# Projection products of 512 columns cut into halves of 256 columns, in a retention and FFN kernel on one core

## The reference

```python
def attention(x, Wq, Wk, Wv, Wg, Wo, gn_weight):      # H = 4 heads, q and k 64 wide, v 128 wide
    q, k = apply_rotary(heads(x @ Wq), heads(x @ Wk))  # x @ Wq and x @ Wk: 256 columns each
    v = heads(x @ Wv)                                  # 512 columns
    o = chunk_retention(q * 64 ** -0.5, k, v, gamma)   # causal, decays by gamma per token
    g = silu(x @ Wg)                                   # 512 columns
    return (rmsnorm(o, gn_weight) * g) @ Wo

def ffn(x, w_gate, w_up, w_down):                      # int weights * 1/127, hidden width 768
    return (silu(x @ w_gate.T) * (x @ w_up.T)) @ w_down.T

x = layernorm(x + attention(x, ...))
x = layernorm(x + ffn(x, ...))
```

## Time and profile before

| what | value |
|---|---|
| median of the 3 runs | 449.24 us |
| the profiled execution: its time, its span | 449.29 us, 447.6 us |
| granted TensorE clock, mean | 0.999 |
| TensorE matmul busy | 434.5 us (97%) |
| TensorE weight loads busy (beside the matmuls) | 392.7 us (88%) |
| VectorE, ScalarE, GpSimd busy | 69%, 60%, 54% |

### The profile page before, as it was taken

The page is one execution under the profiler, slowest core; times in us unless marked ns, Lnnn a source line. Parts: engine busy times, 40 slices in busy tenths (PEclk is TensorE's granted clock), DMA queues, the critical chain, the costliest instruction groups (busy, mean ns, idle before and its releaser), DMA issues.

```text
span 447.6 us, 10332 instructions
## 1 busy us (share of the span) xinstructions
PE 434.5 (97%) x3288; PEld 392.7 (88%) x3288; DVE 307.6 (69%) x785; ACT 269.3 (60%) x794; POOL 241.3 (54%) x381
## 2 busy tenths in 40 slices
PE   8989999999999999999999999999999999999994
PEld 3877889999999999999999999999999999999983
DVE  3989565677666677666768667577766667765774
ACT  5778766566655566654666556556665556665541
POOL 2654355655655466554666436665565536554564
PEclk9999999999999999999999999999999999999999
DMA  7911010010100101010010202002010100100011
GB/s 244 349 42 49 0 49 1 1 61 13 61 12 26 34 12 59 12 59 12 19 39 12 59 12 59 0 12 59 12 59 12 35 1 12 37 14 12 14 38 38
DMA packets 15932, 18.45 MB, mean 41 GB/s; under 512 B 1440, under 2 KB 13728, under 8 KB 15904
## 3 DMA queue, kind: packets, MB, share of 16 engines
q1 hardware_dynamic: 15904, 18.09, 12.7%
HBM read 13.89 MB, written 4.19 MB: 40 GB/s over the span
## 4 chain that ended last, share of the span: by engine, by line
PE 87%; DVE 6%; issue 2%; POOL 1%; ACT 1%; DMA 1%; SPq 0%; POOLq 0%; DVEq 0%; ACTq 0%
PE b_rows L399 44%; PE b_ffn L399 18%; PE b_head L496 6%; PE b_state L399 3%; PE b_head L464 3%; PE b_head L467 3%; PE b_turn L412 3%; PE b_turn L522 3%; PE b_ffn L485 2%; DMA wf_int<-in_w_proj 1%; DVE y L1095 1%; DVE qk L1012 1%; DVE rot_s L999 1%; POOL h_lo L1262 1%; DVE rot_c L992 1%
## 5 line engine op out<-in xcount | busy, mean ns | idle before, releaser
L1262 POOL TENSOR_TENSOR h_lo<-wf_int,h_hi 128x256 fp32r<-128x256 f32 x96 | 71.4, 743 | 61.4 <-ACT h_hi L822 61.0
L399 PE MATMUL b_ffn<-x1T_hi,wf_hi 128*128 128x256 f32 x384 | 92.7, 278 | 0.6 <-DVE x1T_lo L1074 0.6
L399 PE MATMUL b_ffn<-x1T_lo,wf_hi 128*128 128x256 f32 x384 | 91.8, 276 | 0.0
L399 PE MATMUL b_rows<-wp_hi,xT_hi 128*128 128x512 f32 x186 | 78.8, 424 | 0.0
L399 PEld LDWEIGHTS b_ffn<-x1T_hi,wf_hi 128*128 128x128 f32 x384 | 72.1, 188 | 3.9 <-DVE x1T_lo L1074 1.1
L399 PEld LDWEIGHTS b_ffn<-x1T_lo,wf_hi 128*128 128x128 f32 x384 | 72.1, 188 | 2.8
L1287 POOL TENSOR_TENSOR ve<-mv,eps 128x1 f32<-128x1 f32 x64 | 14.1, 221 | 111.7 <-DVE mv L1116 103.9
L399 PE MATMUL b_rows<-wp_hi,xT_lo 128*128 128x512 f32 x186 | 73.4, 395 | 0.0
L399 PE MATMUL b_rows<-wp_lo,xT_hi 128*128 128x512 f32 x186 | 73.3, 394 | 0.0
L786 ACT ACTIVATE sq<-b_head 128x128 f32<-128x128 f32 x124 | 34.5, 278 | 57.2 <-PE b_head L496 54.3
L1107 DVE TENSOR_TENSOR z<-b_rows,x_sb 128x256 f32<-128x256 f32 x32 | 13.6, 424 | 67.0 <-PE b_rows L399 67.0
(11 more groups left out here) (112 smaller groups left out, 1078.2 us busy)
## 6 DMA issues: line engine op xcount, KB each, us to landing
xT_raw<-in_xT SPq DMA_DIRECT2D x16, 256.0 KB, 3.1
x_sb<-in_x SPq DMA_DIRECT2D x16, 256.0 KB, 2.7
out<-wf_int SPq DMA_DIRECT2D x32, 128.0 KB, 1.7
wf_int<-in_w_ffn SPq DMA_DIRECT2D x6, 384.0 KB, 7.0
wf_int<-in_w_proj SPq DMA_DIRECT2D x6, 256.0 KB, 4.8
rope_sb<-in_rope SPq DMA_DIRECT2D x4, 256.0 KB, 6.6
wo_raw<-in_w_o SPq DMA_DIRECT2D x1, 512.0 KB, 7.6
gn_sb<-in_gn SPq DMA_DIRECT2D x1, 0.5 KB, 7.0
```

The source lines that it names most:

```text
L399: mm = pe.matmul(dst, a, b, start=(i == 0 and j == 0 and not begun), stop=(i == n - 1 and j == len(passes) - 1 and not more), skip_group_c ...
L1262: pool.tensor_tensor(h_lo[:, ring, hb], h_full[:, u], h_hi[:, ring, hb].bitcast(F32), ALU.subtract).then_inc(h_split[j], 1)
```

## The change

A new function issues the six passes of a projection. Its first `whole` passes are made over all 512 columns, as before. The other passes are made first for columns 0 to 255 and then for columns 256 to 511. `whole` is 3 for q and k, 0 for v and 3 for g. Slot 0 keeps its own branch.

```diff
+            def projection_passes(dst, stat, mov, whole):
+
+                passes = [(sh if st == 0 else sl, mh if mt == 0 else ml)
+                          for (sh, sl), (mh, ml) in zip(stat, mov) for st, mt in ((0, 0), (0, 1), (1, 0))]
+                n = len(passes)
+                for i in range(whole):
+                    a, b = passes[i]
+                    pe.matmul(dst[:], a, b, start=i == 0, stop=False, skip_group_check=True)
+                for cols in (slice(0, 256), slice(256, 512)):
+                    for i in range(whole, n):
+                        a, b = passes[i]
+                        mm = pe.matmul(dst[:, cols], a, b[:, cols], start=i == 0, stop=i == n - 1,
+                                       skip_group_check=True)
+                return mm
...
                 else:
-                    mm = split_product(dst[:], stat, mov)
+                    mm = projection_passes(dst, stat, mov, (3, 0, 3)[c])
                 mm.then_inc(done, 1)
```

## The result

The changed kernel takes 452.97 us (median of 5 runs, 452.81 to 453.36) against 449.11 us before: a ratio of 1.0083, interval 1.0072 to 1.0094. It is 3.9 us slower, where 2.2 us less had been forecast. Its profiled span is 451.2 us.

The account below looks back on a forecast made before the run. TensorE's matmul stream was taken to bound the kernel: 27 slots x 0.080 = 2.16 us, plus some 0.04 from the first slots, made 2.2 us less, 449.24 - 2.2 = 447.0 us. The range was 446.0 to 449.2.

Parts of the forecast that it names:

- What bounds the kernel: From the first slots on, TensorE's stream of matmuls sets the time; TensorE is busy 97% of the span.
- the first term: In each slot's projections, 12 cut passes at 226.7 ns for two halves against 233.3 whole: 0.080 us gained a slot.
- The size of a cut at the fast pace: In q and k, v and g: timeline gains of 0.02, 0.04 and 0.03 us a slot, together 0.09.
- The part about the drain: The drain at the end has no projection and shifts as a whole.
- Extra weight loads at nothing: The 372 added weight loads in the projections hide behind the pass before them; unhidden, 0.19 us each, 70 us in all.
- The wait for `x1T_split`: Rival: at FFN block 0 a later VectorE chain takes up to all 2.2 us, leaving 449.2 us; chance 0.07.
- the loop's code: Rival: the longer loop body no longer fits on chip, four jumps back fetch, up to 6.8 us, 453.8; chance 0.04.
- the surcharge of the operands: Rival: projection passes' 20 ns belong to their operands: by column 449.2 us, chance 0.06; by instruction 455.7, chance 0.06.
- its turning point: At L417, the halves: the operand surcharge turns the change to slower from 116.7 ns a half on.
- The rule of the Trainium skill: Warm matmuls every N / 2.4 ns and 2.5 ns: two halves 218.3 against 215.8 ns, 0.8 us lost.

Follow-up runs that it names:

- v_only: Changed kernel with all six passes of q and k and of g whole, so only v in halves: 448.65 us, 0.9974 of the kernel before.
- v_and_g: Changed kernel with all six passes of q and k whole, v and g cut as in the change: 447.58 us, 0.9950 of the kernel before.
- v_one_whole: Changed kernel with the first pass of v whole, its other five in halves: 451.90 us, 1.0047 of the kernel before.
- qk_only: Changed kernel with all passes of v and g whole, so only q and k cut: 453.04 us, 1.0067 of the kernel before.
- qk_wide_end: Changed kernel with the last of q and k's six passes whole again, behind two passes in halves: 453.49 us, 1.0097 of the kernel before.
- qk_1_whole: Changed kernel with 1 instead of 3 whole passes in q and k: 452.98 us, 1.0088 of the kernel before.
- fifth_turn: Changed kernel with a fifth matmul in the turn of q and k, repeating the fourth block: 450.92 us, 1.0032 of the kernel before.

## Why the prediction was wrong

- **What bounds the kernel:** right. TensorE's stream sets the time before and after, and the loss from slot 7 to the last turn is in the spacing of its matmuls.
- **The step that failed** is the first term, "By the spacings, a slot gains 12 x (233.3 - 226.7) = 0.080 us". It took 113.3 ns as the cost of a narrow pass wherever it stands, and with that took for granted that the passes behind the halves keep their cost. In the change 52 narrow passes of a slot (46 without a state update) run at 117.7, that is 18 halves and 34 passes that nobody touched. 52 x 4.4 = 0.23 us more, against 0.08 less, gives 0.15, and the slot grew by 0.14. Over four slots, with 12.55 us in place of 12.44 in the fourth, it is 0.13 a slot. It holds for 25 slots and not for 27: at q and k of slot 7 the changed kernel is 0.15 us ahead of the one before (76.35 against 76.51 us), behind the last turn of q and k it is 3.19 behind (412.10 against 408.91). These 3.34 us are most of the 3.65 between the two profiled spans. Another 0.46 lie behind the last matmul, on the other engines; that tail took 6.4 to 7.7 us in the traces looked at, so they are not put down to the change.
- **The size of a cut at the fast pace** was right: 0.04 us a slot for v's six and 0.02 for g's three, as v_only and v_and_g showed. With a whole-pass count that keeps the fast pace, the kernel does come out at 447.0 to 447.6 us, which is what had been forecast for 3, 0, 3. The part about the drain was right too: from the last turn of q and k to the last matmul it is 32.10 us in both traces.
- **Extra weight loads at nothing:** held in v_only, with 186 more of them and a gain. Weight loads are busy 414.2 instead of 392.7 us, 21.5 more and not 14. In v_and_g, at the fast pace, 279 more loads made 11.7 us more (404.4), which would be 15.6 for 372. The other 6 are about what some 1300 narrow passes take longer at 4.4 ns each, an estimate: in a narrow stream the loads run nearly throughout.
- **The wait for `x1T_split` and the loop's code:** right that neither mattered. There is no new wait, and the loop's later rounds fetched no instructions (DMA table, 144 to 358 us, the only row with a queue):

```profile
q1 hardware_dynamic: 6656, 6.29, 9.5%
```

- **The rivals:** the surcharge of the operands came nearest, and its turning point, 116.7 ns a half, was passed. But its mechanism fails: the same operands ran at 113 ns in nine runs, and passes with other operands slowed down as much. None of the rivals had the true one, a cost to passes that the change leaves alone, so the range ended at 449.2.
- **The rule of the Trainium skill** in "TensorE: Matmul & The Clock Gate", section "Back-to-back issue gap", forecast a loss, and a loss came, but not that one. By it a narrow pass is 109.2 ns and two halves lose 2.5 ns to a wide pass; here they won 6.7 at the fast pace and lost 2.1 at the slow one. The prediction also took the rule too widely: that section gives it for a single matmul by itself, and says that a stream of weight loads and matmuls has a spacing of its own.

**What stays open:** why a narrow stream has two paces, and by what state of TensorE the pace is chosen. Shown is only that it is fixed where the stream begins, that it depends on the matmuls before (in slots 7 to 31 on their number behind the turn of q and k, in slot 6 on something from further back), that neither the moved waits nor the other order of passes changed it, that the same halves' operands ran at either pace, that the place in the program doesn't decide (slots 28 to 31, written out, and the four slots of the loop's body have the same pace), and that it lasts until the recall matmuls end the stream. Whole passes inside it brought the fast pace back in v_one_whole and qk_only from slot 7 on, the slow one in slot 5 of v_one_whole, and changed nothing in qk_wide_end. Slot 6 of the change, behind a slow output product, suggests that a state is handed on from stretch to stretch. The pace of the output product alone isn't it: in qk_1_whole it is slow ahead of slot 6 (1.41 us for twelve), and the stream behind one whole pass is slow there, while the same order in slot 7 gave a fast one. No run varied that alone.

## What to carry to other kernels

The spacing of a matmul is no constant of its shape: read it for every stretch of the trace, the drain too, and if a shape shows two values, ask which of them a change will bring to the passes around it. When a small change to TensorE's stream moves the time the wrong way without a new wait, divide the chain's rows by their counts, first of all for the code that was not changed. Then vary the number of wide passes ahead by one: here that alone was worth 5 us of 450. Look at every slot and not at one: the rule by odd and even fits slots 8 to 31 of all these kernels and fails in some before.

## What the runs showed of the hardware

- A stream of 128 x 128 by 128 x 256 float32r matmuls, each with its weight load, at the granted clock of 1.0 (2.4 GHz), runs at 113.3 or at 117.7 ns a matmul, and keeps to one of them for 46 and more. The profile's duration tells them apart as well: 276 ns against 281 for one matmul inside such a stream.
- One more matmul of 0.109 us ahead of it can change the pace of the 52 narrow passes behind it (fifth_turn against the change, 5.9 against 6.1 us).
- 512 columns cost 233 ns on the average, so that two matmuls of 256 columns are cheaper than one of 512 at the fast pace, and dearer at the slow one (226.7 and 235.4 ns).
